# Expert stages: tiles that stay in PSUM, and one transfer for both rows of a unit

## What is computed

```
shared = silu(x @ sg_w.T) * (x @ su_w.T) @ sd_w.T
...
h = silu(einsum('th,eih->eti', x, eg_w)) * einsum('th,eih->eti', x, eu_w)
routed = einsum('eti,ehi,te->th', h, ed_w, comb)
return (shared + routed)
```

## Time and profile before

| | |
|---|---|
| median of 3 runs | 2387.56 us (2387.32 to 2389.07) |
| profiled execution | 2387.65 us, span 2385.8 us |
| stage m0, experts | about 301 to 411 us |
| stage m1, experts | about 634 to 942 us: DVE busy 288.66 us, PE 272.15 us |
| stage m2, experts | about 1140 to 1621 us: DVE busy 473.43 us, PE 437.63 us |

### The profile page before, as it was taken

The page is one execution under the profiler, slowest core; times in us unless marked ns, Lnnn a source line. Parts: engine busy times, 40 slices in busy tenths (PEclk is TensorE's granted clock), DMA queues, the critical chain, the costliest instruction groups (busy, mean ns, idle before and its releaser), DMA issues. The chain is left out here.

```text
span 2385.8 us, 50677 instructions
## 1 busy us (share of the span) xinstructions
PE 1873.4 (79%) x16799; PEld 1167.7 (49%) x16806; DVE 1893.2 (79%) x3977; ACT 1354.8 (57%) x3451; POOL 546.9 (23%) x490
## 2 busy tenths in 40 slices
PE   6999787576688887585899999995777686774987
...
GB/s 73 4 4 4 11 191 118 37 1 0 82 143 132 140 135 50 15 1 11 205 202 202 201 202 202 204 181 15 14 0 13 13 0 13 13 0 28 2 1 19
DMA packets 53549, 172.00 MB, mean 72 GB/s; under 512 B 9136, under 2 KB 34352, under 8 KB 36784
## 3 DMA queue, kind: packets, MB, share of 16 engines
...
## 5 line engine op out<-in xcount | busy, mean ns | idle before, releaser
L810 ACT ACTIVATE m_hwhi<-m_hw 128x512 f16<-128x512 f32 x523 | 326.9, 625 | 209.9 <-DVE m_hw L855 209.8
L836 DVE TENSOR_TENSOR m_hwlo<-m_hw,m_hwhi 128x512 f16<-128x512 f32 x362 | 395.9, 1094 | 0.2
L816 ACT ACTIVATE m_h<-ps 128x512 f32<-128x512 f32 x520 | 308.9, 594 | 74.3 <-PE ps L774 62.7
L747 POOL TENSOR_TENSOR m_hwlo<-m_hw,m_hwhi 128x512 f16<-128x512 f32 x167 | 231.7, 1388 | 456.4 <-ACT m_hwhi L810 407.0
L855 DVE TENSOR_TENSOR m_hw<-m_h,m_comb 128x512 f32<-128x512 f32 x388 | 316.1, 833 | 20.0 <-DMA m_comb<-m_shares 11.3
L780 PE MATMUL ps<-m_hwhi,m_whi 128*128 128x512 f16 x532 | 204.8, 385 | 87.7 <-DVE m_hwlo L836 87.2
L774 PE MATMUL ps<-x_hi,m_whi 128*128 128x512 f16 x652 | 248.9, 382 | 5.2 <-ACTq L805 5.2
L774 PE MATMUL ps<-x_lo,m_whi 128*128 128x512 f16 x652 | 248.8, 382 | 0.0
L774 PE MATMUL ps<-x_hi,m_wlo 128*128 128x512 f16 x652 | 248.6, 381 | 0.0
L780 PE MATMUL ps<-m_hwlo,m_whi 128*128 128x512 f16 x532 | 203.0, 382 | 0.0
L780 PE MATMUL ps<-m_hwhi,m_wlo 128*128 128x512 f16 x532 | 202.8, 381 | 0.0
...
## 6 DMA issues: line engine op xcount, KB each, us to landing
m_comb<-m_shares SPq DMA_DIRECT2D x256, 512.0 KB, 6.4
...
```

The costliest lines, as they stand in the source:

```text
L747: nc.gpsimd.tensor_tensor(hw_lo[:, slot, :], hw[:, n, :], hw_hi[:, slot, :], ALU.subtract)\
L810: nc.scalar.activation(hw_hi[:, k % HB, :], hw[:, n, :], ACT.Copy).then_inc(hi_done, 1)
L816: nc.scalar.activation(h[:, k % 2, :], gate_bank(k), func).then_inc(act_done, 1)
L836: nc.vector.tensor_tensor(hw_lo[:, slot, :], hw[:, n, :], hw_hi[:, slot, :], ALU.subtract)\
```

## The change

A tile keeps its PSUM bank from the first product until its low part is made: ACT applies the function in place (in m1 it still writes `h` in SBUF), DVE multiplies in place, and the high and low parts are read out of the bank. Only where GpSimd makes the low part does DVE write the weighted tile to SBUF (`hw_pool`), since the low part is then made from that copy. In m1 bank 4 alone takes gates and banks 5 to 7 (NB = 3) take ups. Before a product may overwrite a bank, PE waits for the low part of the tile NB before (for a tile of GpSimd, for its weighted copy). The shares of both halves of a unit come in one transfer: a source of 2 rows (1 in m0), each repeated 64 (128) times. The first round of every loop is written out apart, without the work and waits that lag behind nothing, so the zeroing goes.

The core of the diff:

```
     U, _, COLS = weights.shape
-    bodies = U // UB
-    assert bodies * UB == U
-    AHEAD = 2 if gated else 4
-    LAG = 4
+    LAG = NQ
     HB = 2 * UB
+    NB = 3 if gated else 4
     ON_POOL = (1, 3) if gated else (1,)
     ON_DVE = tuple(n for n in range(NQ) if n not in ON_POOL)
     ps = S.psum
     acc = [ps[:, n, :] for n in range(NQ)]
...
-    h, hu, hw = sb("h", [P, 2, QW], F32), sb("hu", [P, 2, QW], F32), sb("hw", [P, 4, QW], F32)
+    h = sb("h", [P, 2, QW], F32) if gated else None
+    hw_pool = sb("hwp", [P, NQ, QW], F32)
+    hw_hi, hw_lo = sb("hwhi", [P, HB, QW], F16), sb("hwlo", [P, HB, QW], F16)
     warm = sb("warm", [P, 1], F32)
-    hw_hi, hw_lo = sb("hwhi", [P, HB, QW], F16), sb("hwlo", [P, HB, QW], F16)
...
-    def gate_bank(k):
-        return ps[:, 4 + (2 * (k % 2) if gated else k % 4), :]
-
-    def up_bank(k):
-        return ps[:, 5 + 2 * (k % 2), :]
-
-    def wait_low(engine, u, n):
...
-        if n in ON_POOL:
-            engine.wait_ge(lo_pool, u * len(ON_POOL) + (ON_POOL.index(n) + 1))
-        else:
-            engine.wait_ge(lo_dve, u * len(ON_DVE) + (ON_DVE.index(n) + 1))
+    def bank(k):
+        return ps[:, 8 - NB + k % NB, :]
+
+    def acted(k):
+        return h[:, k % 2, :] if gated else bank(k)
+
+    def weighted(k):
+        return hw_pool[:, k % NQ, :] if k % NQ in ON_POOL else bank(k)
+
+    def fixed(unit, per, more):
+        return unit * per + more
+
+    def each_body(engine, body):
+
+        body(fixed, lambda each: each, True)
+        with engine.Fori(0, U // UB - 1) as j:
+            body(lambda unit, per, more: j * (UB * per) + ((UB + unit) * per + more),
+                 lambda each: j * each + 2 * each, False)
+
+    def wait_low(engine, at, k):
+
+        s, n = k // NQ, k % NQ
+        lo, own = (lo_pool, ON_POOL) if n in ON_POOL else (lo_dve, ON_DVE)
+        engine.wait_ge(lo, at(s, len(own), own.index(n) + 1))
 
     with nc.Block(no_gpsimd_drain=True) as block:
...
             route.sync(sp)
+
+            def spread(row, s):
+                many = 2 if halves else 1
+                sp.dma_start(comb[:, s, :], route.rows[bass.ds(row, many)].unsqueeze(1)
+                             .broadcast_to([many, P // many, N])).then_inc(comb_got[s], 16)
+
             for s in range(UB):
-                sp.wait_ge(split_done, s + 1)
                 sp.dma_start(stage[:, s, :], weights[s]).then_inc(slot_got[s], 16)
             sp.wait_ge(route.stored, 16 * len(route.turns))
             for s in range(1 if halves else 0, UB):
-                for half in range(2):
-                    row = 2 * (s - 1) + half if halves else s // 2
-                    sp.dma_start(comb[half * 64:half * 64 + 64, s, :], route.rows[row:row + 1].broadcast_to([64, N]))\
-                        .then_inc(comb_got[s], 16)
-            with sp.Fori(0, bodies - 1) as j:
+                spread(2 * (s - 1) if halves else s // 2, s)
+            with sp.Fori(0, U // UB - 1) as j:
                 for s in range(UB):
-                    sp.wait_ge(split_done, j * UB + (UB + s + 1))
+                    sp.wait_ge(split_done, j * UB + (s + 1))
                     sp.dma_start(stage[:, s, :], weights[bass.ds(j * UB + (UB + s), 1)]
                                  .rearrange("u p c -> p (u c)")).then_inc(slot_got[s], 16)
-                    sp.wait_ge(hw_done, j * (4 * UB) + (4 * UB + 4 * s + 4))
-                    for half in range(2):
-                        row = j * (2 * UB) + (2 * (UB + s - 1) + half) if halves else j * (UB // 2) + (UB + s) // 2
-                        sp.dma_start(comb[half * 64:half * 64 + 64, s, :],
-                                     route.rows[bass.ds(row, 1)].broadcast_to([64, N])).then_inc(comb_got[s], 16)
+                    sp.wait_ge(hw_done, j * (NQ * UB) + (NQ * s + NQ))
+                    spread(j * (2 * UB) + 2 * (UB + s - 1) if halves else j * (UB // 2) + (UB + s) // 2, s)
 
...
             if halves:
-                nc.gpsimd.memset(comb[:, 0, :], 1.0).then_inc(comb_got[0], 32)
-
...
+            def low(at, k):
+                pool.wait_ge(hi_done, at(k // NQ, NQ, k % NQ + 1))
+                nc.gpsimd.tensor_tensor(hw_lo[:, k % HB, :], weighted(k), hw_hi[:, k % HB, :], ALU.subtract)\
                     .then_inc(lo_pool, 1)
 
-            with pool.Fori(0, bodies) as j:
+            def body(at, turn, first):
                 for s in range(UB):
-                    u = j * UB + s
-                    pool.wait_ge(down_done, j * (4 * UB) + 4 * s + LAG)
-                    pool.wait_ge(slot_got[s], j * 16 + 16)
+                    if not first:
+                        pool.wait_ge(down_done, at(s - UB, NQ, NQ))
+                    pool.wait_ge(slot_got[s], turn(16))
                     pool.sem_inc(split_start, 1)
                     nc.gpsimd.tensor_copy(w_hi[:, s, :], stage[:, s, :]).then_inc(split_hi, 1)
-                    pool.wait_ge(split_hi, u + 1)
+                    pool.wait_ge(split_hi, at(s, 1, 1))
                     nc.gpsimd.tensor_tensor(w_lo[:, s, :], stage[:, s, :], w_hi[:, s, :], ALU.subtract)\
                         .then_inc(split_done, 1)
                     for n in ON_POOL:
...
-            def down(s, n, slot):
+            def down(k):
                 for a, b in ((w_hi, hw_hi), (w_hi, hw_lo), (w_lo, hw_hi)):
-                    last = nc.tensor.matmul(acc[n], a[:, s, COLS - P:COLS], b[:, slot, :], start=False, stop=False,
-                                            skip_group_check=True)
-                return last.then_inc(down_done, 1)
-
...
-            with pe.Fori(0, bodies) as j:
-                for s in range(UB):
-                    pe.wait_ge(split_done, j * UB + (s + 1 + UB))
-                    for n in range(NQ):
-                        k = 4 * s + n
-                        kk = j * (4 * UB) + k
-                        pe.wait_ge(act_done, kk + (5 - AHEAD))
-                        product(gate_bank(k), slice(0, P), s, n).then_inc(gate_done, 1)
-                        if gated:
-                            pe.wait_ge(hu_done, kk + 1)
-                            product(up_bank(k), slice(P, 2 * P), s, n).then_inc(up_done, 1)
-                        wait_low(pe, j * UB + s, n)
-                        down((s - 1) % UB, n, (k - LAG) % HB)
-            for n in range(NQ):
-                wait_low(pe, U, n)
-                down(UB - 1, n, (4 * U - 4 + n) % HB)
+                    last = nc.tensor.matmul(acc[k % NQ], a[:, k // NQ % UB, COLS - P:COLS], b[:, k % HB, :], start=False,
+                                            stop=False, skip_group_check=True)
+                last.then_inc(down_done, 1)
...
+            def body(at, turn, first):
+                for k in range(NQ * UB):
+                    s, n = k // NQ, k % NQ
+                    if n == 0:
+                        pe.wait_ge(split_done, at(s, 1, 1))
+                    if gated:
+                        if not first or k > 0:
+                            pe.wait_ge(act_done, at(s, NQ, n))
+                        product(ps[:, 4, :], slice(0, P), s, n).then_inc(gate_done, 1)
+                    if not first or k >= NB:
+                        gone = k - NB
+                        if gone % NQ in ON_POOL:
+                            pe.wait_ge(hw_done, at(gone // NQ, NQ, gone % NQ + 1))
+                        else:
+                            wait_low(pe, at, gone)
+                    if gated:
+                        product(bank(k), slice(P, 2 * P), s, n).then_inc(up_done, 1)
+                    else:
+                        product(bank(k), slice(0, P), s, n).then_inc(gate_done, 1)
+                    if not first or k >= LAG:
+                        wait_low(pe, at, k - LAG)
+                        down(k - LAG)
...
-            nc.scalar.activation(warm[:], hw[:, 0, 0:1], func)
-
-            def high(k, n):
-                nc.scalar.activation(hw_hi[:, k % HB, :], hw[:, n, :], ACT.Copy).then_inc(hi_done, 1)
...
+            nc.scalar.activation(warm[:], S.ident[:, 0:1], func)
+
+            def high(k):
+                nc.scalar.activation(hw_hi[:, k % HB, :], weighted(k), ACT.Copy).then_inc(hi_done, 1)
+
+            def body(at, turn, first):
+                for k in range(NQ * UB):
+                    s, n = k // NQ, k % NQ
+                    act.wait_ge(gate_done, at(s, NQ, n + 1))
+                    nc.scalar.activation(acted(k), ps[:, 4, :] if gated else bank(k), func).then_inc(act_done, 1)
+                    if not first or k > 0:
+                        act.wait_ge(hw_done, at(s, NQ, n))
+                        high(k - 1)
+
...
-            def low(u, n, slot):
-                dve.wait_ge(hi_done, u * 4 + (n + 1))
-                nc.vector.tensor_tensor(hw_lo[:, slot, :], hw[:, n, :], hw_hi[:, slot, :], ALU.subtract)\
+
+            def low(at, k):
+                dve.wait_ge(hi_done, at(k // NQ, NQ, k % NQ + 1))
```

(30 more changed lines are left out.)

66 lines of the change are left out of this document (19 added, 47 removed).

## The result

The changed kernel takes 3919.11 us (median of four runs, 3916.86 to 3920.61) against 2388.32 for the kernel before, measured beside it (2387.32 to 2391.18): a ratio of 1.6406, with a 95% interval of 1.6377 to 1.6434.

The account below looks back on a forecast made before the run. Share transfers on two DMA engines were taken to bound m1 and m2, with PE, ACT and DVE waiting: 2387.65 - 6 (m0) + 368.7 (m1) + 1172.4 (m2) = 3922.8 us; likeliest 3922, range 3800 to 4500.

Parts of the forecast that it names:

- Two engines for m1's and m2's shares: Transfers to comb: a source of 2 pieces outermost uses 2 of 16 DMA engines, 130 packets per transfer; chance 0.75.
- 26.0 GB/s per engine: Transfers to comb in m1 and m2: each engine moves 524,288 bytes at 26.0 GB/s, 20.2 us.
- All transfers on the same two engines: Transfers to comb in m1 and m2 do not overlap; a unit costs 20.6 us in m1, 20.5 in m2.
- rival (d): m1 and m2: two engines, but another pair for each transfer, one landing every 6.9 us; 2490 us, chance 0.02.
- m1 +368.7, m2 +1172.4: Added stage times: 32 transfers of 20.6 us in m1, 80 of 20.5 in m2, plus landing and tail.
- m0 -6: Stage m0: 4 us off the start by the single transfer and 2 us from shorter units.
- the chain: Held PSUM banks, product to freed bank: 2.85 us in m0 and m2, unit 5.70; 3.02 in m1, unit 9.92.
- The price of part 1: Tiles kept in PSUM hold banks: m1 loses 25 us, m2 wins 12, m0 2; hidden while transfers bind.
- rival (a): Transfers to comb use sixteen engines after all and held banks bind; 2395 us, chance 0.10.
- Rival (b): Sixteen engines, m1's chain hidden by PE's queue of gate products, PE bounds all stages; 2275 us, chance 0.05.
- the landing of the loads to comb: Profile row of the one-MB loads: landing about 20 us or more, against 6.4 before.
- SP's later load of weights: SP's wait delays its next load of weights, which then comes some 20 us before its use: hidden.

Follow-up runs that it names:

- e3: The changed kernel with the one transfer's source written as 64 repeats of the pair of rows, repeats outermost; 2383.83 us, ratio 0.9985.
- e4: The changed kernel with a source of 8 rows each repeated 16 times in m1, 4 rows each repeated 32 times in m2; 2788.64 us.
- e8: The changed kernel with a source of 16 rows each repeated 8 times in m1, 8 rows each repeated 16 times in m2; 2417.49 us.
- e10: The changed kernel with a source of 4 rows each repeated 32 times in m1, 16 rows each repeated 8 times in m2; 2419.36 us.
- e1: The changed kernel with its held banks and peeled round, but the two rows brought by two transfers over 64 partitions as before; 2389.24 us, ratio 1.0004.
- e7: e1 with three PSUM banks in place of four in m2; 2724.03 us in one run.
- e5: e1 with DVE's low part of a tile behind the multiply of the next tile instead of the one after; 2299.24 us, ratio 0.9634.

## Why the prediction was right

3922 us was predicted, 3919.11 measured. The mechanism held at each step, but that the total is off by under 4 us is in part luck: against the sum m1 came 2.2 us longer, m2 3.0 shorter and the rest 5 shorter. Step by step:

- **Two engines for m1's and m2's shares** held: 130 packets per transfer, 15% of the DMA engines. e3, which has the same bytes, rows and partitions, shows that it is the order of the source's dimensions; e4, e8 and e10 show that 4, 8 and 16 pieces use 4, 8 and 16 engines. The Trainium skill's rule that the prediction weighed (DMA: Bandwidth & Descriptors, Why a DMA increments its semaphore by 16 and not by 1), the largest number up to 16 that divides both outermost sizes, gives the same numbers for all of these, 2 to 64 pieces.
- **26.0 GB/s per engine** held. From the first issue to the last landing m2 has (3140.30 - 1502.31 - 1.7) / 80 = 20.45 us per transfer for 20.5, m1 (1288.29 - 626.07 - 1.7) / 32 = 20.64 for 20.6. The low end, 12.9 GB/s, belonged to another case: every layout that ran near 14 GB/s had 8 or 16 engines at work.
- **All transfers on the same two engines** held; rival (d) would have landed one every 6.9 us (its own working, 20.5 / 3, gives 6.8, which would take 5 us off its 2490).
- **m1 +368.7, m2 +1172.4** came as +370.9 and +1169.4. The tails were 15.1 us for 14.2 and 11.0 for 10.3, taken from the kernel before, where DVE was never starved.
- **m0 -6** came as -6.3 to its copies: the first multiply waited until 307.60 instead of 311.39, 3.8 us for the 4 taken, for which the prediction gave no working, and the rest is the shorter unit. The other stages gave some 5 us more, which the sum had at nothing; I have no cause for them, and stretches between the same two points differed by up to 4 us from kernel to kernel. The prediction named m0's unit as the sign of the chain, with 5.70 us; in the changed kernel it is 343.34 - 337.70 = 5.64 us:

```profile
337.70 0.70 DVE L859 TENSOR_TENSOR ps<-ps,m_comb 128x512 f32<-128x512 f32 x1 [0.82 <-ACT ps L826]
...
343.34 0.70 DVE L859 TENSOR_TENSOR ps<-ps,m_comb 128x512 f32<-128x512 f32 x1 [0.73 <-ACT ps L826]
```

- **The price of part 1**, hidden in the result, was rival (a) by itself. The sum for part 1 alone was 2399 (rival (a)'s 2395 without the 4 us of m0's transfer) and e1 gave 2389: m1 was right to 1 us, m0 and m2 were each 3 us better than worked out (a step is 2.82 us and not 2.85, and 160 steps make 5 us), and 2 to 3 us lie outside the stages. e7 and e5 let the chain span fewer and more tiles, and the times followed to within 0.1 and 5.3 us. Rival (b) asked for a shorter step and named PE's queue as what would hide it; e1 shows that the queue doesn't. In e5 another order on DVE does, by laying the same chain over three tiles.
- **The DVE rows**: 0.68 to 0.70 us each, none at 1.64. GpSimd's low part fell from 1.26 in the earlier trace rows to 1.15.
- **A sign that could not be read** as written, the landing of the loads to comb: the page gives a landing time of 5.0 us for comb, since only m0's sixteen transfers have one; the 20 us show in the spacing of DVE's waits.
- **SP's later load of weights** was hidden, as said, but its issue is no longer short. SP's timeline in m2:

```profile
1973.56 18.81 SPq L736 DMA_DIRECT2D m_stage<-in_m_w  x1
1992.62 0.61 SPq L725 DMA_DIRECT2D m_comb<-m_shares  x1
1993.79 5.33 SPq L736 DMA_DIRECT2D m_stage<-in_m_w  x1
2002.53 13.24 SPq L725 DMA_DIRECT2D m_comb<-m_shares  x1
2016.04 17.45 SPq L736 DMA_DIRECT2D m_stage<-in_m_w  x1
```

Over the whole kernel an issue of weights inside the loop takes SP 17.7 us in the median and 21.5 at most, against 0.37 and 0.53 in the kernel before and 0.37 and 0.93 in e3, which issues the same transfers in the same order. So the length goes with the slow transfers ahead; by what means they hold SP, no row shows. The weights land 42 us after their issue (6.0 before), and GpSimd still has them 20 us before DVE's next unit at 2016.17:

```profile
1996.08 0.40 POOL L757 CAST m_whi<-m_stage 128x256 f16<-128x256 f32 x1 [15.68 <-DMA m_stage<-in_m_w]
```
